# Last layer norm of a decoder layer: variance of four blocks computed on GpSimd over three slots, and a dequantisation factor in one operation

## Chip, cores and metric

One core of a Trainium2 chip runs the whole kernel in one launch. The metric is the device time of one execution in microseconds (us). Engines are named as in the profile: PE is TensorE (PEld its weight loads), DVE is VectorE, ACT is ScalarE, POOL is GpSimd, SP is SyncE, which here issues the DMAs.

## The reference, cut to what matters

The input is x (64, 64, 256) float32, so 4096 tokens of 256 values. Three parts follow each other, each with a residual and a layer norm. The change lies in the third:

```python
def _quant_weight(w):
    scale = jnp.mean(jnp.abs(w)) + EPS
    return jnp.clip(jnp.round(w / scale), -1.0, 1.0) * scale

def _quant_act(x):
    scale = jnp.maximum(jnp.max(jnp.abs(x), axis=-1, keepdims=True), EPS) / 127.0
    return jnp.clip(jnp.round(x / scale), -128.0, 127.0) * scale

def bitlinear(x, w):
    return jnp.einsum('bsi,oi->bso', _quant_act(x), _quant_weight(w))

x = _layernorm(x + self_attention(x))
x = _layernorm(x + cross_attention(x, ctx))
gate = sigmoid(bitlinear(x, w_gate))          # 256 -> 1024
h = gate * bitlinear(x, w_up)                 # 256 -> 1024
x = _layernorm(x + bitlinear(h, w_down))      # 1024 -> 256
# _layernorm(x) = (x - mean) / sqrt(var + 1e-5), over the 256 values of a token
```

## The kernel before

The tokens lie in SBUF as X, 32 blocks of 128 tokens (a token per partition) by 256 values. Self-attention and cross-attention run first (functions self_attention and cross_attention, about 1366 us of the span). The feed-forward (function feed_forward, from L1431) is the rest, and the change touches it alone.

It is written as one program per engine. Each is a loop over 36 slots (blocks, L1470), and in slot n an engine does the pieces of several blocks: has(k) says that block n-k exists. All orders are written out by hand; every engine works its own list strictly in that order, and a wait on a semaphore stops all that is behind it on that engine.

For block n the pieces are: PE multiplies into gP and uP (L1487, slot n); ACT takes the sigmoid of gP (sig, L1529, slot n); DVE multiplies by uP (hs, L1630), takes the largest magnitude (hsc, L1633) and its reciprocal (hinv, L1635), all in slot n; POOL limits hinv (L1581), quantises to hm (L1584) and makes the dequantisation factor dsc in two steps (L1585, L1587), in slot n; PE transposes hm (L1506) and ACT copies it out as hqT (L1540) in slot n+2; PE multiplies with the down weights into xprojP (L1497, called dP in the code), ACT scales that by dsc (ds, L1535) and POOL adds it to X (L1578) in slot n+3; DVE takes the norm's statistics (L1665, a count, a mean and a sum of squares for the even and the odd values) and aggregates them to mean and variance (ln_moments, L1667) in slot n+4. The last three blocks are scaled and added by DVE (L1661).

The normalisation works on groups of four blocks. POOL's roots (L1564 to L1571) makes 1/sqrt(var + eps) and minus mean times that, for the four blocks at once, in the slot in which the fourth is aggregated: for blocks 4m to 4m+3 that is slot 4m+7. ACT normalises block e in slot e+10 (L1554), as its last piece in that slot, after hqT of block n-2 and ahead of the next slot's sig. The first block of a group, 4m, is therefore normalised in slot 4m+10:

```python
NORMED = [[e for e in range(MAIN) if min(e + 10, NB + 3) == n] for n in range(NB + 4)]
for e in NORMED[n]:
    wait(act, s_shift, e // GROUP + 1)
```

MAIN is 28: blocks 28 to 31 form two groups of their own (28 to 30, and 31), normalised by DVE at the end (L1678). Blocks 28 to 31 also pass the norm of the cross-attention here, since their last projection ends as the feed-forward starts: DVE's L1638 to L1652, POOL's L1591 to L1603, and ACT's L1550, in slots 1 to 13. SP sends each finished group to the output (L1620).

DVE may write hs of block n once POOL's hm of block n-2 is done; PE may write uP of block n once hs of n-1 is done, and gP of n once sig of n-1 is done.

Of the kernel before, what the change touches and what calls it, by code (L numbers as in the profile page):

```python
# [5 lines left out]
F32 = mybir.dt.float32  # L6
# [1424 lines left out]
def feed_forward(nc, X, ffn, projP, out, sem, sb, part):  # L1431
# [11 lines left out]
    s_g, s_u, s_t, s_dn = (sem("f_" + n) for n in ("g", "u", "t", "dn"))  # L1443
    s_sig, s_h, s_max, s_sc, s_inv, s_dsc, s_hm, s_te, s_ds, s_y = (sem("f_" + n) for n in (
        "sig", "h", "max", "sc", "inv", "dsc", "hm", "te", "ds", "y"))
    s_stats, s_mom, s_rstd, s_normed, s_out = (sem("f_" + n) for n in ("stats", "mom", "rstd", "normed", "out"))
# [28 lines left out]
    with nc.Block() as block:  # L1475
# [46 lines left out]
        def _(act):  # L1522
            def slot(n, has):
# [35 lines left out]
        @block.gpsimd  # L1559
        def _(pool):  # L1560
            def roots(m):
                own = groups[m]
                wait(pool, s_mom, own.stop)
                nc.gpsimd.tensor_scalar(rstd[:, own], moments[:, own, 1], EPS, None, ALU.add).then_inc(s_small, 1)  # L1564
                wait(pool, s_small, 2 * m + 2 - max(0, m - MAIN // GROUP))
                nc.gpsimd.tensor_tensor(rstd[:, own], rstd[:, own], power[:, 0:own.stop - own.start], ALU.pow).then_inc(s_rstd, 1)
                if own.stop <= MAIN:
                    nc.gpsimd.tensor_scalar(shift[:, own], moments[:, own, 0], -1.0, None, ALU.mult).then_inc(s_small, 1)
                    wait(pool, s_small, 2 * m + 3)
                    wait(pool, s_rstd, m + 1)  # L1570
                    nc.gpsimd.tensor_tensor(shift[:, own], shift[:, own], rstd[:, own], ALU.mult).then_inc(s_shift, 1)  # L1571

            def slot(n, has):
# [5 lines left out]
                if has(0):  # L1579
                    wait(pool, s_inv, n + 1)  # L1580
                    nc.gpsimd.tensor_scalar(hinv[:, n:n + 1], hinv[:, n:n + 1], 1.0 / EPS, 127.0, ALU.min, ALU.mult).then_inc(s_sc, 1)  # L1581
                    wait(pool, s_sc, 2 * n + 1)
                    wait(pool, s_t, n - 1)
                    nc.gpsimd.tensor_scalar(hm[:, n % 2, :], hs[:, n % 2, :], hinv[:, n:n + 1], MAGIC16, ALU.mult, ALU.add).then_inc(s_hm, 1)  # L1584
                    nc.gpsimd.tensor_scalar(hsc[:, n:n + 1], hsc[:, n:n + 1], EPS, 1.0 / 127.0, ALU.max, ALU.mult).then_inc(s_sc, 1)  # L1585
                    wait(pool, s_sc, 2 * n + 2)
                    nc.gpsimd.tensor_tensor(dsc[:, n:n + 1], hsc[:, n:n + 1], wsc[:, 2:3], ALU.mult).then_inc(s_dsc, 1)  # L1587
                if n == 5:
# [35 lines left out]
        def _(dve):  # L1624
            def slot(n, has):
                if has(0):
                    wait(dve, s_sig, n + 1)
                    wait(dve, s_u, n + 1)
                    wait(dve, s_hm, n - 1)
                    nc.vector.scalar_tensor_tensor(hs[:, n % 2, :], uP[:, :], usc[:, n:n + 1], sig[:, n % 2, :],  # L1630
                                                   ALU.mult, ALU.mult).then_inc(s_h, 1)
                    wait(dve, s_h, n + 1)
                    nc.vector.tensor_reduce(hsc[:, n:n + 1], hs[:, n % 2, :], AX, ALU.max, apply_absolute_value=True).then_inc(s_max, 1)  # L1633
                    wait(dve, s_max, n + 1)
                    nc.vector.reciprocal(hinv[:, n:n + 1], hsc[:, n:n + 1]).then_inc(s_inv, 1)  # L1635
                if 1 <= n < 1 + PB:
# [94 lines left out]
```

## Time and profile before

| | us |
|---|---|
| median of 3 runs (lowest, highest) | 1492.27 (1491.41, 1496.97) |
| the profiled execution's own time | 1494.54 |
| its span | 1492.8 |
| mean granted clock of TensorE in it | 0.986 |
| busy over the span: PE, DVE, ACT, POOL | 1408.2, 1197.6, 1255.8, 1270.1 |
| of 1438 to 1452 us (14 us, in the feed-forward): PE, DVE, ACT, POOL | 14.00, 13.52, 12.87, 11.88 |

The profile is one execution, recorded per instruction; its times are counted from the start of the span. A timeline row gives the start, the duration, the engine, the line and what is written from what; a duration of an instruction in flight overlaps the next, so the cost of one on its engine is the distance from its start to the next one's start. "[1.96 <-ACT sig L1529]" behind a row means that its engine had stood idle for 1.96 us until that one finished.

### The profile page before, as it was taken

Reading aid. Unit: us, or ns where it says so; the run is one execution under the profiler, and the core shown is the slowest. Engines: PE = TensorE matmul, PEld = TensorE weight load, DVE = VectorE, ACT = ScalarE, POOL = GpSimd, SP = SyncE. Lnnn points to the kernel's source line nnn. Section 1 sums busy time; section 2 is a strip of 40 time slices with the busy share of each in tenths; the row PEclk is TensorE's granted clock in tenths of the full one; section 3 lists DMA queues with packets and bytes.
Section 4 is the critical chain, followed back from the end, with each engine's and each line's share of the span. In section 5 each row is a group of like instructions: output and inputs, shape, how many; then the busy total and the mean of one; then the engine's idle time right before and its main releaser. Section 6 shows DMA issues by size and latency. Waiting matters only on the chain. (4 is left out here: it accounts for less than half of the span.)

```text
span 1492.8 us, 54232 instructions
## 1 busy us (share of the span) xinstructions
PE 1408.2 (94%) x20034; PEld 1035.4 (69%) x20034; DVE 1197.6 (80%) x2796; ACT 1255.8 (84%) x4059; POOL 1270.1 (85%) x1307
## 2 busy tenths in 40 slices
PE   6999999999999999999999999778999999987897
PEld 4677777777777777777777777636777777765564
DVE  5887887887888878878877778777888888874997
ACT  6888888888888888888888887668999999995787
POOL 6989999999889889899898897657888899883887
PEclk9999999999999999999999999899999999998999
DMA  7700000000000000000000000022434433330012
GB/s 256 199 3 31 31 3 30 31 3 31 21 13 30 3 31 31 3 31 31 3 17 16 3 3 3 5 82 83 114 110 113 111 94 97 98 86 1 1 43 72
DMA packets 58133, 73.27 MB, mean 49 GB/s; under 512 B 14320, under 2 KB 41776, under 8 KB 57872
## 3 DMA queue, kind: packets, MB, share of 16 engines
q1 hardware_dynamic: 57872, 69.79, 15.6%
q8 instruction: 163, 2.67, 0.8%
q14 instruction: 98, 0.80, 0.2%
HBM read 32.54 MB, written 4.19 MB: 25 GB/s over the span
## 5 line engine op out<-in xcount | busy, mean ns | idle before, releaser
L652 DVE SCALAR_TENSOR_TENSOR X<-projP,r,X 128x256 f32<-128x256 f32 x512 | 211.2, 475 | 2.4 <-PE projP L333 2.3
L302 PEld LDWEIGHTS svP<-W,xT 128*128 128x128 bf16 x3072 | 182.2, 98 | 30.5 <-DVE scores L639 0.7
L256 PE MATMUL qkssP<-xT,W 128*128 128x512 bf16 x768 | 189.2, 383 | 9.2 <-POOL W L730 8.0
L725 POOL TENSOR_TENSOR y_sql<-y_sq 128x512 bf16<-128x512 f32 x128 | 133.5, 1043 | 71.5 <-ACT y_sq L457 71.2
L302 PE MATMUL svP<-W,xT 128*128 128x128 bf16 x3072 | 192.4, 219 | 0.0
L256 PE MATMUL kP<-xT,W 128*128 128x512 bf16 x768 | 186.9, 379 | 0.2 <-DVE kl L693 0.2
L333 PE MATMUL projP<-W,y 128*128 128x256 bf16 x1024 | 176.6, 275 | 2.1 <-POOL yl L725 2.1
L1216 ACT ACTIVATE x_probs<-xsP,x_ntop 128x64 f32<-128x64 f32 x512 | 152.2, 324 | 25.9 <-DVE x_ntop L1293 25.1
L472 ACT ACTIVATE probs<-scores,ntop 128x64 f32<-128x64 f32 x512 | 170.5, 339 | 3.7 <-DVE ntop L642 3.5
L725 POOL TENSOR_TENSOR k_sql<-moved_k 128x512 bf16<-128x512 f32 x128 | 135.8, 1061 | 19.2 <-ACT moved_k L483 18.1
L924 POOL TENSOR_TENSOR qhl<-qh 128x1024 bf16<-128x1024 f32 x64 | 121.2, 1893 | 33.3 <-issue 26.0
L765 POOL TENSOR_TENSOR KVl<-q 128x512 bf16<-128x512 f32 x128 | 145.6, 1137 | 0.0
L333 PE MATMUL projP<-W,yl 128*128 128x256 bf16 x512 | 140.5, 274 | 0.0
L256 PEld LDWEIGHTS kP<-xT,W 128*128 128x128 bf16 x768 | 75.2, 98 | 91.6 <-issue 0.8
L768 POOL TENSOR_TENSOR vl<-v 128x512 bf16<-128x512 f32 x128 | 135.6, 1059 | 0.7 <-DVE v L669 0.7
L725 POOL TENSOR_TENSOR q_sql<-turned_k 128x512 bf16<-128x512 f32 x128 | 133.1, 1040 | 2.9 <-ACT turned_k L464 2.9
L725 POOL TENSOR_TENSOR yl<-y 128x512 bf16<-128x512 f32 x128 | 133.1, 1040 | 0.0
L256 PEld LDWEIGHTS qkssP<-xT,W 128*128 128x128 bf16 x768 | 64.9, 98 | 77.1 <-issue 10.4
L669 DVE COPY v<-svP 128x512 f32<-128x512 f32 x128 | 88.3, 690 | 31.7 <-PE svP L302 31.2
L639 DVE SCALAR_TENSOR_TENSOR scores<-svP,r,bias 128x64 f32<-128x64 f32 x512 | 110.0, 277 | 4.5
L688 DVE TENSOR_TENSOR ptl<-pyP,pth 128x256 bf16<-128x256 f32 x128 | 54.3, 424 | 73.7 <-ACT pth L497 71.4
L1216 ACT ACTIVATION_READ_ACCUMULATOR x_probs<-xsP,x_ntop 128x1 f32 x512 | 111.4, 218 | 0.0
(277 smaller groups left out, 4934.6 us busy)
## 6 DMA issues: line engine op xcount, KB each, us to landing
x_turned<-x_turn SPq DMA_DIRECT2D x128, 128.0 KB, 2.1
oB<-oA SPq DMA_DIRECT2D x232, 64.0 KB, 2.0
w_stage<-in_wqkvp SPq DMA_DIRECT2D x16, 512.0 KB, 3.5
x_stage<-in_xT SPq DMA_DIRECT2D x8, 512.0 KB, 4.1
X<-in_x SPq DMA_DIRECT2D x1, 4096.0 KB, 16.9
x_stage<-in_ctxT SPq DMA_DIRECT2D x8, 512.0 KB, 4.4
out<-X SPq DMA_DIRECT2D x7, 512.0 KB, 2.9
okv<-in_L_xattn_W_o SPq DMA_DIRECT2D x1, 2048.0 KB, 11.5
```

The lines of the kernel that those rows point to most:

```text
L256: last = nc.tensor.matmul(dst[:, :], weight(parity, u, i, c), xT[:, z, c, tok], start=(c == 0 and k == 0), stop=(c == CC - 1 and k == 2))
L302: last = nc.tensor.matmul(svP[:, b * D:(b + 1) * D], xT[:, u, c, t * TILE + b * P:t * TILE + (b + 1) * P], weight(parity, z, 2, c), start= ...
L333: last = nc.tensor.matmul(projP[:, b * C:(b + 1) * C], y_part, W[:, (j - 3) // NT % 2, z, 3 * CC * D:], start=(i == 0), stop=(i == 2))
L472: last = nc.scalar.activation(probs[:, b, :], scores[:, b, :], ACT.Exp, bias=ntop[:, b:b + 1], accum_out=total[:, b:b + 1])
L639: last = nc.vector.scalar_tensor_tensor(scores[:, b, :], svP[:, b * T:(b + 1) * T], r[:, b:b + 1], row, ALU.mult, ALU.add)
L652: last = nc.vector.scalar_tensor_tensor(acc, projP[:, b * C:(b + 1) * C], r[:, PB + b:PB + b + 1], acc, ALU.mult, ALU.add)
L669: nc.vector.tensor_copy(v[:, j % 4, :], svP[:, :]).then_inc(s_ve, 1)
L725: return nc.gpsimd.tensor_tensor(dst[:, :], src[:, :], high(src, slice(None), 0, TILE), ALU.subtract)
L765: nc.gpsimd.tensor_tensor(ql[:, j % 2, :], q[:, j % 2, :], high_of(q, j % 2), ALU.subtract).then_inc(s_ql, 1)
L768: nc.gpsimd.tensor_tensor(vl[:, j % 4, :], v[:, j % 4, :], high_of(v, j % 4), ALU.subtract).then_inc(s_vl, 1)
L924: return eng.tensor_tensor(dst, src, high_part(src), ALU.subtract)
L1216: last = nc.scalar.activation(probs[:, m % 3, b % PB, b // PB, :], sP[:, b * T:(b + 1) * T], ACT.Exp, bias=ntop[:, b:b + 1], accum_out=tot ...
```

## The change

DVE no longer aggregates blocks 0 to 27 (L1667 remains for 28 to 31). POOL makes their variance out of the two halves' means and sums of squares: with M the mean of the even values, N of the odd, and S and T their sums of squares, 4 (var + eps) = (S + T) 4/C + 4 eps + (M - N)^2. For a group of four blocks this takes ten operations of 128x4, in three pieces: sums (three) in slot 4m+7, variances (four) in slot 4m+8, and roots (three) in slot 4m+9, which ends with the doubling of rstd that ACT's normalisation now waits for. ACT's list is as it was; the semaphore count that it waits for is that of the last operation of roots. Besides, 1/127 is multiplied into the weight's scale once (wdc), so that dsc takes one operation with two steps instead of two operations, in every slot. DVE's two semaphores of max and reciprocal become one that counts both.

```diff
+    gap, wdc = sb("ln3_gap", [P, NB], F32), sb("wdc", [P, 1], F32)
...
                 for e in NORMED[n]:
                     x = X[:, e, :]
-                    wait(act, s_shift, e // GROUP + 1)
+                    wait(act, s_shift, 2 * (e // GROUP + 1))
                     nc.scalar.activation(x, x, ACT.Identity, bias=shift[:, e:e + 1], scale=rstd[:, e:e + 1]).then_inc(s_by_act, 1)
...
+            def sums(m):
+                own = groups[m]
+                st = stats[:, own, :]
+                wait(pool, s_stats, own.stop)
+                nc.gpsimd.tensor_tensor(gap[:, own], st[:, :, 1], st[:, :, 4], ALU.subtract).then_inc(s_small, 1)
+                nc.gpsimd.tensor_tensor(shift[:, own], st[:, :, 1], st[:, :, 4], ALU.add).then_inc(s_small, 1)
+                nc.gpsimd.tensor_tensor(rstd[:, own], st[:, :, 2], st[:, :, 5], ALU.add).then_inc(s_small, 1)
+
+            def variances(m):
+                own = groups[m]
+                wait(pool, s_small, 7 * m + 5)
+                nc.gpsimd.tensor_scalar(rstd[:, own], rstd[:, own], 4.0 / C, 4.0 * EPS, ALU.mult, ALU.add).then_inc(s_small, 1)
+                nc.gpsimd.tensor_tensor(gap[:, own], gap[:, own], gap[:, own], ALU.mult).then_inc(s_small, 1)
+                nc.gpsimd.tensor_scalar(shift[:, own], shift[:, own], -1.0, None, ALU.mult).then_inc(s_small, 1)
+                wait(pool, s_small, 7 * m + 8)
+                nc.gpsimd.tensor_tensor(rstd[:, own], rstd[:, own], gap[:, own], ALU.add).then_inc(s_small, 1)
+
             def roots(m):
                 own = groups[m]
-                wait(pool, s_mom, own.stop)
-                nc.gpsimd.tensor_scalar(rstd[:, own], moments[:, own, 1], EPS, None, ALU.add).then_inc(s_small, 1)
...
+                wait(pool, s_small, 7 * m + 9)
+                nc.gpsimd.tensor_tensor(rstd[:, own], rstd[:, own], power[:, :], ALU.pow).then_inc(s_rstd, 1)
+                wait(pool, s_rstd, m + 1)
+                nc.gpsimd.tensor_tensor(shift[:, own], shift[:, own], rstd[:, own], ALU.mult).then_inc(s_shift, 1)
+                wait(pool, s_shift, 2 * m + 1)
+                nc.gpsimd.tensor_scalar(rstd[:, own], rstd[:, own], 2.0, None, ALU.mult).then_inc(s_shift, 1)
...
                 if has(0):
-                    wait(pool, s_inv, n + 1)
+                    wait(pool, s_top, 2 * n + 2)
...
-                    nc.gpsimd.tensor_scalar(hsc[:, n:n + 1], hsc[:, n:n + 1], EPS, 1.0 / 127.0, ALU.max, ALU.mult).then_inc(s_sc, 1)
-                    wait(pool, s_sc, 2 * n + 2)
-                    nc.gpsimd.tensor_tensor(dsc[:, n:n + 1], hsc[:, n:n + 1], wsc[:, 2:3], ALU.mult).then_inc(s_dsc, 1)
+                    nc.gpsimd.tensor_scalar(dsc[:, n:n + 1], hsc[:, n:n + 1], EPS, wdc[:, 0:1], ALU.max, ALU.mult).then_inc(s_dsc, 1)
...
                 for m in range(NG):
-                    if n - 4 == groups[m].stop - 1:
-                        roots(m)
+                    end = groups[m].stop - 1
+                    if end < MAIN:
+                        for lag, part_ in enumerate((sums, variances, roots)):
+                            if n - 4 - lag == end:
+                                part_(m)
+                    elif n - 4 == end:
+                        last_roots(m)
...
+            nc.gpsimd.tensor_scalar(wdc[:, :], wsc[:, 2:3], 1.0 / 127.0, None, ALU.mult).then_inc(s_small, 1)
...
                     nc.vector.bn_stats(stats[:, e, :], X[:, e, :]).then_inc(s_stats, 1)
-                    wait(dve, s_stats, e + 1)
-                    nc.vector.bn_aggr(moments[:, e, :], stats[:, e, :]).then_inc(s_mom, 1)
+                    if e >= MAIN:
+                        wait(dve, s_stats, e + 1)
+                        nc.vector.bn_aggr(moments[:, e, :], stats[:, e, :]).then_inc(s_mom, 1)
```

POOL's list before, from its last operation of slot 7 to the end of slot 8, with the first group's roots between (X<-ds,X opens a slot; dsc closes its part for the block):

```order
L1587 TENSOR_TENSOR dsc<-hsc,wsc 128x1 [waits f_sc]
L1564 TENSOR_SCALAR ln_rstd<-ln_moments 128x4 [waits f_mom]
L1566 TENSOR_TENSOR ln_rstd<-ln_rstd,ln_power 128x4 [waits f_small]
L1568 TENSOR_SCALAR ln_shift<-ln_moments 128x4
L1571 TENSOR_TENSOR ln_shift<-ln_shift,ln_rstd 128x4 [waits f_rstd,f_small]
L1578 TENSOR_TENSOR X<-ds,X 128x256 [waits f_ds]
L1581 TENSOR_SCALAR hinv<-hinv 128x1 [waits f_inv]
L1584 TENSOR_SCALAR hm<-hs,hinv 128x1024 [waits f_t,f_sc]
L1585 TENSOR_SCALAR hsc<-hsc 128x1
L1587 TENSOR_TENSOR dsc<-hsc,wsc 128x1 [waits f_sc]
```

POOL's list of the change over the end of slot 8 and slot 9, where the same group's second and third pieces stand (its sums stand at the end of slot 7):

```order
L1611 TENSOR_SCALAR hm<-hs,hinv 128x1024 [waits f_t,f_sc]
L1612 TENSOR_SCALAR dsc<-hsc,wdc 128x1
L1576 TENSOR_SCALAR ln_rstd<-ln_rstd 128x4 [waits f_small]
L1577 TENSOR_TENSOR ln_gap<-ln_gap 128x4
L1578 TENSOR_SCALAR ln_shift<-ln_shift 128x4
L1580 TENSOR_TENSOR ln_rstd<-ln_rstd,ln_gap 128x4 [waits f_small]
L1605 TENSOR_TENSOR X<-ds,X 128x256 [waits f_ds]
L1608 TENSOR_SCALAR hinv<-hinv 128x1 [waits f_top]
L1611 TENSOR_SCALAR hm<-hs,hinv 128x1024 [waits f_t,f_sc]
L1612 TENSOR_SCALAR dsc<-hsc,wdc 128x1
L1586 TENSOR_TENSOR ln_rstd<-ln_rstd,ln_power 128x4 [waits f_small]
L1588 TENSOR_TENSOR ln_shift<-ln_shift,ln_rstd 128x4 [waits f_rstd]
```

The last operation that ACT needs of the group (L1590, behind the row shown last) now stands behind the hm of two more slots than L1571 did.

ACT's list before, which the change leaves in this order, around the end of slot 9 and slot 10 (the row of L1554 is the first block of the first group):

```order
L1550 ACTIVATE X<-X,ln_shift,ln_rstd 128x256 [waits f_lastp]
L1529 ACTIVATE sig<-gP,gsc 128x1024 [waits f_h,f_g]
L1535 ACTIVATE ds<-xprojP,dsc 128x256 [waits f_y,f_dsc,f_dn]
L1540 ACTIVATE hqT<-hmP 128x1024 [waits f_dn,f_t]
L1554 ACTIVATE X<-X,ln_shift,ln_rstd 128x256 [waits f_shift]
```

Nothing moved there; the next row on ACT is the sig of slot 11.

## Rows read from the trace of the kernel before

**Rows 1.** Chain that ended last, a slot of the feed-forward: start, us, engine, what, line

```profile
1439.19 1.29 DVE hs L1630
...
1441.76 0.16 DVE hinv L1635
...
1442.39 1.30 DVE hs L1630
```

**Rows 2.** Timeline of DVE, the slot before: start us, us, engine, line, op, out<-in

```profile
1438.64 0.41 DVE L1665 BATCH_NORM_STATS2 ln_stats<-X 128x6 f32<-128x256 f32 x1
1439.08 0.18 DVE L1667 BATCH_NORM_AGGREGATE ln_moments<-ln_stats 128x2 f32<-128x6 f32 x1
```

**Rows 3.** Timeline of PE, first and fifth of the groups of one slot

```profile
1422.87 1.03 PE L1487 MATMUL gP<-wg,xqT 128*128 128x512 bf16 x4
...
1425.92 0.61 PE L1516 MATMUL hmP<-identh,f_xs 128*128 128x128 f16 x8
```

**Rows 4.** Timeline of POOL, slot 9 (an ordinary slot)

```profile
1406.14 0.72 POOL L1578 TENSOR_TENSOR X<-ds,X 128x256 f32<-128x256 f32 x1
1406.94 0.22 POOL L1581 TENSOR_SCALAR hinv<-hinv 128x1 f32<-128x1 f32 x1
1407.26 1.12 POOL L1584 TENSOR_SCALAR hm<-hs,hinv 128x1024 f16<-128x1024 f32 x1
1408.46 0.22 POOL L1585 TENSOR_SCALAR hsc<-hsc 128x1 f32<-128x1 f32 x1
1408.77 0.19 POOL L1587 TENSOR_TENSOR dsc<-hsc,wsc 128x1 f32<-128x1 f32 x1
1408.91 0.72 POOL L1578 TENSOR_TENSOR X<-ds,X 128x256 f32<-128x256 f32 x1
```

**Rows 5.** Timeline of POOL, roots of the first group, end of slot 7

```profile
1401.37 0.25 POOL L1564 TENSOR_SCALAR ln_rstd<-ln_moments 128x4 f32<-128x4 f32 x1
1401.70 1.04 POOL L1566 TENSOR_TENSOR ln_rstd<-ln_rstd,ln_power 128x4 f32<-128x4 f32 x1
1402.83 0.26 POOL L1568 TENSOR_SCALAR ln_shift<-ln_moments 128x4 f32<-128x4 f32 x1
1403.17 0.20 POOL L1571 TENSOR_TENSOR ln_shift<-ln_shift,ln_rstd 128x4 f32<-128x4 f32 x1
```

**Rows 6.** Timeline of ACT and DVE: block 0's normalisation in slot 10, then slot 11

```profile
1407.63 0.59 ACT L1554 ACTIVATE X<-X,ln_shift,ln_rstd 128x256 f32<-128x256 f32 x1
1408.12 1.10 ACT L1529 ACTIVATE sig<-gP,gsc 128x1024 f32<-128x1024 f32 x1
...
1409.38 1.28 DVE L1630 SCALAR_TENSOR_TENSOR hs<-uP,usc,sig 128x1024 f32<-128x1024 f32 x1
```

**Rows 7.** Timeline of ACT, DVE, POOL: the last tile's norm, slots 6 and 7

```profile
1394.93 0.60 ACT L1550 ACTIVATE X<-X,ln_shift,ln_rstd 128x256 f32<-128x256 f32 x1 [2.05 <-POOL ln_shift L1596]
...
1396.57 1.28 DVE L1630 SCALAR_TENSOR_TENSOR hs<-uP,usc,sig 128x1024 f32<-128x1024 f32 x1 [1.96 <-ACT sig L1529]
...
1399.39 0.23 POOL L1581 TENSOR_SCALAR hinv<-hinv 128x1 f32<-128x1 f32 x1 [0.99 <-DVE hinv L1635]
```

**Rows 8.** Timeline of DVE and POOL: hs of slots 12 and 15, f_xs in slot 12

```profile
1414.62 1.28 DVE L1630 SCALAR_TENSOR_TENSOR hs<-uP,usc,sig 128x1024 f32<-128x1024 f32 x1
...
1419.67 1.05 POOL L1603 TENSOR_SCALAR f_xs<-X,xinv 128x256 f16<-128x256 f32 x2
...
1425.62 1.28 DVE L1630 SCALAR_TENSOR_TENSOR hs<-uP,usc,sig 128x1024 f32<-128x1024 f32 x1 [0.32 <-ACT sig L1529]
```

**Rows 9.** Busy time by stretch (us, PE, PEld, DVE, ACT, POOL, then PE's granted clock, DMA)

```profile
1413.90:1415.97 2.07, 0.05 (x2) 0.01 (x1) 1.97 (x6) 1.73 (x3) 1.55 (x5) 1.00 0.00 0
...
1418.20:1419.20 1.00, 1.00 (x10) 0.88 (x9) 1.00 (x1) 0.50 (x2) 0.92 (x2) 0.50 0.00 0
...
1396.60:1398.00 1.40, 1.12 (x5) 0.39 (x6) 1.36 (x2) 1.40 (x3) 1.24 (x4) 1.00 0.00 0
```

**Rows 10.** Timeline of DVE: the last hs, slot 31

```profile
1478.05 1.28 DVE L1630 SCALAR_TENSOR_TENSOR hs<-uP,usc,sig 128x1024 f32<-128x1024 f32 x1
```

More of the change, by code:

```diff
@@ L1443, in feed_forward @@
     s_g, s_u, s_t, s_dn = (sem("f_" + n) for n in ("g", "u", "t", "dn"))
-    s_sig, s_h, s_max, s_sc, s_inv, s_dsc, s_hm, s_te, s_ds, s_y = (sem("f_" + n) for n in (
-        "sig", "h", "max", "sc", "inv", "dsc", "hm", "te", "ds", "y"))
+    s_sig, s_h, s_top, s_sc, s_dsc, s_hm, s_te, s_ds, s_y = (sem("f_" + n) for n in (
+        "sig", "h", "top", "sc", "dsc", "hm", "te", "ds", "y"))
     s_stats, s_mom, s_rstd, s_normed, s_out = (sem("f_" + n) for n in ("stats", "mom", "rstd", "normed", "out"))
@@ L1564, in roots, with last_roots @@
+            def last_roots(m):
+                own = groups[m]
+                wait(pool, s_mom, own.stop - MAIN)
                 nc.gpsimd.tensor_scalar(rstd[:, own], moments[:, own, 1], EPS, None, ALU.add).then_inc(s_small, 1)
-                wait(pool, s_small, 2 * m + 2 - max(0, m - MAIN // GROUP))
+                wait(pool, s_small, 7 * (MAIN // GROUP) + 3 + m - MAIN // GROUP)
                 nc.gpsimd.tensor_tensor(rstd[:, own], rstd[:, own], power[:, 0:own.stop - own.start], ALU.pow).then_inc(s_rstd, 1)
[L1567 to L1571, printed above, removed]
@@ L1579, in slot @@
                 if has(0):
-                    wait(pool, s_inv, n + 1)
+                    wait(pool, s_top, 2 * n + 2)
                     nc.gpsimd.tensor_scalar(hinv[:, n:n + 1], hinv[:, n:n + 1], 1.0 / EPS, 127.0, ALU.min, ALU.mult).then_inc(s_sc, 1)
-                    wait(pool, s_sc, 2 * n + 1)
+                    wait(pool, s_sc, n + 1)
                     wait(pool, s_t, n - 1)
                     nc.gpsimd.tensor_scalar(hm[:, n % 2, :], hs[:, n % 2, :], hinv[:, n:n + 1], MAGIC16, ALU.mult, ALU.add).then_inc(s_hm, 1)
-                    nc.gpsimd.tensor_scalar(hsc[:, n:n + 1], hsc[:, n:n + 1], EPS, 1.0 / 127.0, ALU.max, ALU.mult).then_inc(s_sc, 1)
-                    wait(pool, s_sc, 2 * n + 2)
-                    nc.gpsimd.tensor_tensor(dsc[:, n:n + 1], hsc[:, n:n + 1], wsc[:, 2:3], ALU.mult).then_inc(s_dsc, 1)
+                    nc.gpsimd.tensor_scalar(dsc[:, n:n + 1], hsc[:, n:n + 1], EPS, wdc[:, 0:1], ALU.max, ALU.mult).then_inc(s_dsc, 1)
                 if n == 5:
@@ L1604, in slot @@
                 for m in range(NG):
-                    if n - 4 == groups[m].stop - 1:
-                        roots(m)
+                    end = groups[m].stop - 1
[5 more added lines that the diff above has]
+                        last_roots(m)
             nc.gpsimd.memset(power[:, :], -0.5).then_inc(s_small, 1)
-            pool.wait_ge(s_small, 1)
+            nc.gpsimd.tensor_scalar(wdc[:, :], wsc[:, 2:3], 1.0 / 127.0, None, ALU.mult).then_inc(s_small, 1)
+            pool.wait_ge(s_small, 2)
             blocks(slot, 4)
@@ L1632, in slot @@
                     wait(dve, s_h, n + 1)
-                    nc.vector.tensor_reduce(hsc[:, n:n + 1], hs[:, n % 2, :], AX, ALU.max, apply_absolute_value=True).then_inc(s_max, 1)
-                    wait(dve, s_max, n + 1)
-                    nc.vector.reciprocal(hinv[:, n:n + 1], hsc[:, n:n + 1]).then_inc(s_inv, 1)
+                    nc.vector.tensor_reduce(hsc[:, n:n + 1], hs[:, n % 2, :], AX, ALU.max, apply_absolute_value=True).then_inc(s_top, 1)
+                    wait(dve, s_top, 2 * n + 1)
+                    nc.vector.reciprocal(hinv[:, n:n + 1], hsc[:, n:n + 1]).then_inc(s_top, 1)
                 if 1 <= n < 1 + PB:
```

## The prediction, made before the changed kernel had run

> **What bounds it now.** I read the page first: over the whole span PE is busiest, but the change touches only the feed-forward, so I cut that stage out. The chain of waits runs there through DVE alone in nearly every slot: hs at 1439.19, the reciprocal at 1441.76, the next hs at 1442.39 [rows 1]. A slot is thus 3.20 us, and DVE sets it. The timelines of the engines say how near the others are. PE needs 3.05 us when it waits for nothing (first gP at 1422.87, the fifth group at 1425.92 [rows 3]). POOL needs 2.77 us for an ordinary slot (1406.14 to 1408.91 [rows 4]) and once in four slots the roots: 1401.37 to 1403.17, and about 0.15 for the last of them, 1.95 us [rows 5]. So four slots cost POOL 4 x 2.77 + 1.95 = 13.03 us, against DVE's 12.80. **POOL is already slightly over DVE**, and only the one block by which hm may lag hides it.
>
> The last view is the one that decides: ACT's list. Block 0 is normalised at 1407.63, then comes sig of slot 11 at 1408.12, and DVE's hs of slot 11 at 1409.38 [rows 6]. The shift that this needs was written at 1403.37 (1403.17 + 0.20 [rows 5]), 4.26 us earlier. The normalisation stands in front of a sig, and sig feeds DVE. What happens when it is late is to be seen once: in slot 6 it waited 2.05 us for POOL's shift, and DVE's hs stood idle 1.96 us for the sig behind it [rows 7].
>
> **Part 1: 28 aggregates leave DVE.** Statistics start at 1438.64, the aggregate at 1439.08 [rows 2], the next hs at 1439.19 [rows 1]. Without the aggregate, hs could start 0.33 after the statistics (0.41, less the 0.08 by which independent DVE instructions overlap: hs starts 0.11 after the start of an aggregate of 0.18). DVE gains 0.22 a slot and needs 2.98. PE's 3.05 then stops it, so at most 0.15 a slot is to be had.
>
> **Part 2: dsc in one operation.** hsc and dsc take 0.31 + 0.14 = 0.45 (1408.46, 1408.77, 1408.91 [rows 4]). One operation of hsc's kind takes 0.30; if its end overlapped the next as dsc's does, 0.17. I take 0.30, since the two-step operations in the rows (hinv, hm, hsc) all show their whole duration and 0.08 behind it. It saves 0.15 a slot on POOL, 0.28 at best. The new wdc at the start is one such operation, at a time when POOL has nothing to do; the new waits of the kernel's start cost nothing.
>
> **Part 3: ten operations for four on POOL.** The power costs 1.13 (1401.70 to 1402.83 [rows 5]). Three operations with constants cost 0.33 each, 0.99 (1401.37 to 1401.70). Of the six with two tensors five are followed by one that does not need their result: 0.15 each, as dsc [rows 4]; the sixth, the shift, is waited for: 0.28 (0.20 and 0.08). That is 1.13 + 0.99 + 0.75 + 0.28 = 3.15 us a group, against 1.95. They read strided statistics, which no row shows; the upper bound is 0.28 for all six, 3.80 us. POOL's four slots become 4 x 2.62 + 3.15 = 13.63 us: it saved 0.60 and got 1.20.
>
> The Trainium skill speaks against this on its own ground: GPSIMD Engine Reference, section 3 (Performance versus the Vector engine), says that elementwise work belongs on VectorE, because a GpSimd instruction passes two software dispatch hops. The rows give it right here in the balance: 4 x 0.22 = 0.88 us off DVE for 1.20 us onto POOL. The rule alone would move the kernel by POOL's rate only, which is the first rival below.
>
> **Part 4: where roots now ends.** Follow POOL from the hinv of slot 7, whose time DVE sets: 1399.39 [rows 7]. The slots before it lose 0.37 (one aggregate 0.22 and one dsc 0.15 on that way), so 1399.02. From there POOL does hinv, hm, dsc (0.32 + 1.20 + 0.30 = 1.82), sums (0.45), slot 8 (X 0.80 + 1.82 = 2.62), variances (0.33 + 0.15 + 0.33 + 0.15 = 0.96), slot 9 (2.62), and roots to the end of the doubling (1.13 + 0.28 + 0.25 = 1.66): 10.13 us, which ends at **1409.15**. ACT would reach block 0 at 1407.63 at the latest. So it waits some 1.5 us or more. Behind the wait stand sig of slot 11, then hs on DVE, then uP of slot 12 on PE, then hinv and hm on POOL. hs of slot 11 starts 0.03 + 0.49 (normalisation to sig [rows 6]) + 1.13 (sig to hs, 0.03 the handover: as rows 7, where the ACT starts 0.03 after POOL's end) later, at 1410.80 against 1409.38: **+1.42 us**.
>
> This closes a ring, and the ring is longer than the slots it replaces. From the end of one group's roots to the end of the next: 0.03 + 0.49 + 1.13, then hs to the end of the reciprocal and over to POOL 2.76 (1439.19 to 1441.76 + 0.16 [rows 1], + 0.03), then POOL's 10.13. Sum **14.54 us per four slots**, against 12.80. From hs of slot 11 to that of slot 31 there are five such rings.
>
> The trace has 68.67 us there (1409.38 to 1478.05 [rows 6, 10]). Now: 5 x 14.54 = 72.70. In the first of them the f_xs of slots 12 and 13 come on POOL's way, 2 x 1.14 (1.05 + 0.09) = 2.28 [rows 8]. DVE's extra work in slot 11 (hs to hs 5.24 instead of 3.20 [rows 6, 8]) makes hinv of slot 12 ready 2.98 + 2.04 + 2.76 = 7.78 after hs of slot 11, when POOL is there at 2.76 + 1.82 + 0.45 + 0.80 = 5.83: 1.95 more. In the second, ACT's copy of the last tile delays a sig; I take 0.7 of its 0.9. Sum 72.70 + 2.28 + 1.95 + 0.7 = 77.63: **+8.96 us**. The tail after the last hs hardly changes: I take -0.2. The last group's roots end about a microsecond later, and their output is sent before the last one, which hides it; uncovered it would cost that microsecond.
>
> **The clock** of PE is the open term. After an idle stretch of 2.07 us it fell from 2.4 to 1.2 GHz (granted clock 0.50), and it did not fall after the 1.56 us ahead of 1396.6 [rows 9]. The rings leave PE idle about 1.6 us each, and the first, with DVE's and POOL's extra work, more. While low, PE's groups took 1.65 us more (gP 1.71 from start to start against 0.87, and less for the two before it); part of it is hidden by the ring. I add **1.0 us** for one such fall.
>
> Sum: 1.42 + 8.96 - 0.2 + 1.0 = **+11.2 us**. Against the profiled execution's own 1494.5 us that is 1505.7. This execution lies 2.3 us over the median of 1492.3, so for the median I say 1503.5 us, and 1504 rounded up for the strided reads.
>
> **Rivals.** What a measurement of this kernel can tell from no change is about 0.5%, 7.5 us.
>
> *POOL's rate alone (chance 0.10).* If ACT's wait were met in time, POOL would set the pace with 13.63 us per four slots, 0.83 over DVE's 12.80: over five to six groups 4 to 5 us, less what hm's lag absorbs at the start, so +3 to +4, or 1496. Against it: to be in time roots would have to end 1.5 us earlier, and all durations on that way are measured ones. This also covers the case that small POOL operations overlap much more than in the rows.
>
> *The gain comes through (0.03).* If the ten operations ran closely packed in POOL's gaps, at 0.1 each beside the power, POOL would need 4 x 2.5 + 2.0 = 12.0, and roots would end before ACT asks. The pace would be PE's 3.05, 0.15 under now, over 24 slots: -3.6 us, and 1488.7. It decides from the point at which POOL's way of 10.13 us falls below 8.6. No small row is as short as 0.1.
>
> *The clock falls in every ring (0.22).* The stalls of 1.6 us lie just under the one of 2.07 after which it fell. At 1.65 us a fall, half to all of it in the way, five falls add 4 to 8 us, less the 1.0 taken: 1507 to 1511. The Trainium skill bears on this: TensorE: Matmul & The Clock Gate, section HAM oscillation, says that a wait which comes back in every step makes the array start cold in every step, so that the price is paid each time. By it this rival would be the forecast; the row without a fall after 1.56 us keeps it below.
>
> **Numbers.** The forecast's own chance is 0.65: its lower bound is dsc at 0.17 (three on the ring, six rings, -2.3 us) and no fall (-1.0), so +8 us, 1500; its upper one is 0.28 for five more operations (six rings x 0.65 = +3.9), 1508. I give 1497 to 1511, which takes in the clock's rival and the upper part of POOL's rate. Slower by over 0.5% begins at 1499.7: forecast and clock, less a little for the low edge and the scatter of 1491.4 to 1497.0 in the runs, 0.83. Within 0.5%: 0.15. Faster: 0.02.
>
> **What the profile will show.** Right: in slots 10, 14, 18, 22, 26 and 30 the ACT row X<-X,ln_shift,ln_rstd waits 1.5 to 2.5 us for POOL's ln_rstd, and the hs of the next slot waits for sig; hs to hs is near 3.0 in three slots and about 5.3 in the fourth; the chain passes through POOL's hm, DVE no longer fills it. dsc reads 0.30 from start to start, the ten operations about 3.15. Wrong: no idle time ahead of ACT's normalisation, or a four-slot period under 13.2 us. If the period is 14.5 and the total is off, the clock's row in each stall tells the rest.

## The result, and the profile after

| | before | with the change |
|---|---|---|
| median, us (runs) | 1492.65 (4) | 1511.43 (4) |
| lowest, highest | 1491.41, 1496.97 | 1510.78, 1512.68 |
| profiled execution: own time, span | 1494.54, 1492.8 | 1512.68, 1509.2 |
| the same pair once more, on another chip, medians | 1496.15 (11) | 1510.19 (5) |

The ratio is 1.0112 with a 95% interval of 1.0090 to 1.0134; on the second chip it is 1.0098 (1.0083 to 1.0114). The change made the kernel slower, by 18.8 us in the first pair and by 14.0 in the second. The four runs of each kernel in the first pair do not overlap (1497.0 is the highest before, 1510.8 the lowest after).

The chain that ended last, by engine and by line, from the page of each kernel. DVE led it before:

```profile
DVE 5%; PE 1%; POOL 1%; issue 1%; ACT 0%; DVEq 0%; ACTq 0%; POOLq 0%
```

POOL leads it now:

```profile
POOL 5%; issue 2%; DVE 1%; PE 1%; ACT 0%; DVEq 0%; POOLq 0%; ACTq 0%
POOL hm L1611 2%; POOL X L1605 1%; POOL dsc L1612 1%; POOL hinv L1608 0%; POOL ln_rstd L1586 0%; PE xprojP L1498 0%; DVE hs L1661 0%; POOL f_xs L1628 0%; DVE hsc L1664 0%; ACT hqT L1541 0%; PE hmP L1507 0%; PE uP L1488 0%; POOL ln_shift L1578 0%; POOL ln_rstd L1590 0%; PE gP L1488 0%
```

The waits of the changed kernel from 1403 to 1493 us (engine and line, for whom, us in total, times, longest). ACT's normalisation waited for nothing before; now it waits six times, and the six sigs behind it are what DVE and PE wait for:

```profile
DVE hs L1661 <- ACT sig L1530: 18.9, 12, 4.8
ACT X L1555 <- POOL ln_rstd L1590: 14.8, 6, 4.6
...
PE gP L1488 <- ACT sig L1530: 9.7, 5, 2.7
POOL hinv L1608 <- DVE hinv L1666: 7.9, 7, 1.5
```

The first of these waits, in POOL's, ACT's and DVE's timelines. It stands where [rows 6] showed none:

```profile
1410.38 1.04 POOL L1586 TENSOR_TENSOR ln_rstd<-ln_rstd,ln_power 128x4 f32<-128x4 f32 x1
1411.49 0.20 POOL L1588 TENSOR_TENSOR ln_shift<-ln_shift,ln_rstd 128x4 f32<-128x4 f32 x1
1411.79 0.25 POOL L1590 TENSOR_SCALAR ln_rstd<-ln_rstd 128x4 f32<-128x4 f32 x1
...
1412.07 0.60 ACT L1555 ACTIVATE X<-X,ln_shift,ln_rstd 128x256 f32<-128x256 f32 x1 [2.16 <-POOL ln_rstd L1590]
1412.58 1.09 ACT L1530 ACTIVATE sig<-gP,gsc 128x1024 f32<-128x1024 f32 x1
...
1413.70 1.29 DVE L1661 SCALAR_TENSOR_TENSOR hs<-uP,usc,sig 128x1024 f32<-128x1024 f32 x1 [2.45 <-ACT sig L1530]
```

Roots end at 1412.04; 0.03 later ACT starts, 0.51 after that sig, 1.12 later hs. This is the hand-over that the last tile had shown in [rows 7], now in slots 10, 14, 18, 22, 26 and 30. The second wait is the longest, 4.55 us: the f_xs of slots 12 and 13 and DVE's extra work of slot 11 lie on POOL's way to it. The other five are 1.57 to 2.19 us.

**Where the loss lies.** The medians differ by 18.8 us, the two profiled executions by 18.1. I cut these two at DVE's addition of the last projection (the first row of the feed-forward on DVE, 1368.94 before and 1371.16 after), at hs of slot 0, 7, 11 and 31, and at the end. Every number is a difference of two starts of rows:

| stretch, us | before | changed | difference |
|---|---|---|---|
| start to the addition (no instruction differs) | 1368.94 | 1371.16 | +2.22 |
| addition to hs of slot 0 | 3.18 | 3.64 | +0.46 |
| hs 0 to hs 7 | 24.45 | 24.07 | -0.38 |
| hs 7 to hs 11 | 12.81 | 14.83 | +2.02 |
| hs 11 to hs 31, by fours | 16.24, 13.57, 12.82, 12.81, 13.23 | 18.89, 15.48, 14.82, 14.87, 14.83 | +10.22 |
| hs 31 to the end of the span | 14.75 | 16.61 | +1.86 |
| own time beyond the span | 1.74 | 3.48 | +1.74 |

The feed-forward itself (all but the first and the last row) is +14.18 us. The other 4 us lie outside it: 2.2 ahead of it, where no instruction differs, and 1.7 between the span and the execution's own time.

### The profile page after: what moved, and what is told of

It reads as the page before. It is cut to its first block and busy times, and to the rows that moved or that the text cites. A ratio compares the mean times of both kernels' runs of the same rounds, so it can differ in the third digit from the quotient of the medians.

```text
span 1509.2 us, 54004 instructions
## 1 busy us (share of the span) xinstructions
PE 1385.1 (92%) x19830; PEld 1037.3 (69%) x20034; DVE 1192.6 (79%) x2768; ACT 1255.5 (83%) x4059; POOL 1274.3 (84%) x1318
## 5 line engine op out<-in xcount | busy, mean ns | idle before, releaser
L256 PE MATMUL qkssP<-xT,W 128*128 128x512 bf16 x641 | 161.5, 383 | 29.9 <-issue 20.5
## 6 DMA issues: line engine op xcount, KB each, us to landing
x_turned<-x_turn SPq DMA_DIRECT2D x128, 128.0 KB, 2.1
```

Of the source, the lines that this page charges most:

```text
L256: last = nc.tensor.matmul(dst[:, :], weight(parity, u, i, c), xT[:, z, c, tok], start=(c == 0 and k == 0), stop=(c == CC - 1 and k == 2))
```

## The experiments

They ran in three series, each on a chip of its own. The kernel before has medians of 1497.45, 1496.15 and 1496.82 us there, about 4 us over the first pair's, so each run is compared with the kernel before that ran with it. First series: ACT's normalisation in slots e+11 and e+9 and the two halves alone (21 runs of the kernel before). Second: the change again, the two closer placements, the aggregates kept (11 runs). Third: the late aggregates and the factor alone again (29 runs). "Period" is the distance between the hs of slots 19 and 23, in the trace of each.

| run | ratio to before (95%) | median less before's | period | idle before ACT's normalisation |
|---|---|---|---|---|
| the kernel before | | | 12.82 | 0 |
| the change again | 1.0098 (1.0083 to 1.0114) | +14.0 | 14.82 | 14.8 |
| normalise in slot e+11 | 1.0025 (1.0016 to 1.0033) | +3.0 | 13.77 | 1.3 |
| normalise in slot e+9 | 1.0271 (1.0255 to 1.0287) | +41.6 | 19.63 | 34.3 |
| pieces all in slot 4m+7 | 1.0030 (1.0018 to 1.0043) | +4.6 | 13.87 | 1.1 |
| pieces in slots 4m+7, 4m+8 | 1.0039 (1.0026 to 1.0051) | +5.8 | 13.86 | 4.0 |
| slot e+11, aggregates kept | 1.0033 (1.0021 to 1.0045) | +4.4 | 13.79 | 0.8 |
| the norm's half alone | 1.0101 (1.0086 to 1.0116) | +15.3 | 15.35 | 16.7 |
| the factor's half alone | 0.9981 (0.9972 to 0.9989) | -2.9 | 12.82 | 0 |
| the factor alone, again | 0.9986 (0.9976 to 0.9996) | -1.9 | 12.81 | 0 |
| factor, and a late aggregate | 0.9986 (0.9975 to 0.9997) | -3.0 | 12.57 | 0 |
| late aggregate, old factor | 1.0006 (0.9996 to 1.0016) | +0.7 | 12.57 | 0.3 |

**The change once more.**

> The change itself, again, beside the kernel before on the chip of this series. In its first trace the feed-forward, from the last projection's addition to the end, took 138.04 us against 123.86, +14.2; the rest of the +18.8 us lay ahead of it (+2.2, where no instruction differs) and around the span. If that rest is chance of the execution and the chip, the pair differs here by 13 to 16 us; if it belongs to the change, by 18 to 20 again.

It is +14.0 us, and in its trace the feed-forward takes 138.3 us against 138.0 in the first (14.84, 18.89, 15.60, 14.82, 14.87, 14.82 from hs 7 to hs 31). That is the lower of the two expectations: 14 us belong to the change. What lay outside the feed-forward in the first pair did not come back; the addition starts anywhere between 1368.9 and 1373.2 in the traces of this study, whatever the kernel.

**ACT normalises one slot later.**

```diff
-            NORMED = [[e for e in range(MAIN) if min(e + 10, NB + 3) == n] for n in range(NB + 4)]
+            NORMED = [[e for e in range(MAIN) if min(e + 11, NB + 3) == n] for n in range(NB + 4)]
```

> The change, with ACT normalising block e one slot later (slot e+11). The work of all engines is the same. Ring theory (ACT waits for roots ahead of a sig): the ring loses one POOL slot of 2.6 us and falls from 14.83 to about 12.2 us per four slots, so it no longer sets the pace; no idle time ahead of ACT's normalisation of blocks 4m. POOL's own work then sets it, by the rows after the change 4 x 2.62 + 0.47 + 1.17 + 1.63 = 13.75 us per four slots, so about 1497 us, 14 us under the change, still 4 over the kernel before. Rival, POOL's load or the clock carries the loss and the wait is only where it shows: the order on ACT is of no account, 1509 to 1512 us. Second rival, the gain comes through once the wait is gone: under 1491.

The order of 28 instructions on ACT alone takes 11 of the 14 us away: +3.0 (I had expected +4). Nothing in the lists of DVE or POOL is different, so POOL's load did not carry those 11 us; it carries at most the 3 that are left. And the period is the predicted one, 13.75 expected and 13.76 to 13.77 measured. POOL's timeline of this kernel shows why: from the X that opens the slot after one group's roots to the same of the next it never stands idle (the ordinary slots between are left out, each 2.62 us):

```profile
1455.84 0.73 POOL L1605 TENSOR_TENSOR X<-ds,X 128x256 f32<-128x256 f32 x1
...
1461.10 0.20 POOL L1567 TENSOR_TENSOR ln_gap<-ln_stats 128x4 f32<-128x4 f32 x1
...
1463.92 0.30 POOL L1612 TENSOR_SCALAR dsc<-hsc,wdc 128x1 f32<-128x1 f32 x1
1464.30 0.20 POOL L1576 TENSOR_SCALAR ln_rstd<-ln_rstd 128x4 f32<-128x4 f32 x1
1464.58 0.20 POOL L1577 TENSOR_TENSOR ln_gap<-ln_gap 128x4 f32<-128x4 f32 x1
1464.87 0.24 POOL L1578 TENSOR_SCALAR ln_shift<-ln_shift 128x4 f32<-128x4 f32 x1
1465.19 0.20 POOL L1580 TENSOR_TENSOR ln_rstd<-ln_rstd,ln_gap 128x4 f32<-128x4 f32 x1
...
1467.96 1.04 POOL L1586 TENSOR_TENSOR ln_rstd<-ln_rstd,ln_power 128x4 f32<-128x4 f32 x1
1469.08 0.20 POOL L1588 TENSOR_TENSOR ln_shift<-ln_shift,ln_rstd 128x4 f32<-128x4 f32 x1
1469.37 0.24 POOL L1590 TENSOR_SCALAR ln_rstd<-ln_rstd 128x4 f32<-128x4 f32 x1
1469.59 0.73 POOL L1605 TENSOR_TENSOR X<-ds,X 128x256 f32<-128x256 f32 x1
```

1455.84 to 1469.59 is 13.75 us. DVE and PE now wait for POOL's hm, which is the second wait that the change brings once the first is gone. The waits of the same kernel from 1440 to 1481 us:

```profile
PEld hmP L1507 <- POOL hm L1611: 4.0, 5, 1.2
DVE hs L1661 <- POOL hm L1611: 3.6, 3, 1.2
```

**ACT normalises one slot earlier**, with e + 9 in the same line.

> The change, with ACT normalising block e one slot earlier (slot e+9). Ring theory: the ring grows by one POOL slot of 2.62 us, from 14.83 to 17.45 us per four slots; five rings and the first wait give 6 x 2.6 = 15.7 us, so 1527 us. If TensorE's clock also falls in each wait (they become 4.5 us), up to 1.65 us a ring come on top: 1527 to 1535. Rival, POOL's load carries the loss: no more than 1513 us.

The direction and the growth are the ring's, and a loss of +41.6 us has no place in the rival. The expectation of 1527 to 1535 was built on the first pair's change. Over the kernel before it is +34 to +42, which 41.6 just meets, but over the change it is +16 to +24, and measured against the change (+14.0) it is +27.6. The step from the change's rings to these explains that: 3.35, 3.75, 5.15, 4.81, 5.17 and 5.44 us from hs 7 to hs 31, together 27.7, where 2.62 each was to come from POOL's slot. The last three rings are 19.63 to 20.27 us instead of 17.45. The rest is PE. It stood idle for about 5 us in each ring (7.70 in the second), its clock fell each time, and then the chain ran through it. The chain in one ring (start us, us, what), and the granted clock (last but two) of two stretches of it:

```profile
1457.19 1.03 PE gP L1488 x2
...
1458.44 0.63 PE gP L1488
1459.08 1.71 PE uP L1488 x4
1460.78 1.23 PE xprojP L1498 x8
```

```profile
1457.00:1458.00 1.00, 0.81 (x2) 0.28 (x3) 0.83 (x1) 1.00 (x3) 0.42 (x1) 0.50 0.00 0
...
1459.00:1460.00 1.00, 1.00 (x4) 0.33 (x3) 0.97 (x3) 0.88 (x1) 0.00 (x1) 0.50 0.00 0
```

gP, uP and xprojP take 1.89 + 1.70 + 1.26 = 4.85 us there from gP's start to ds on ACT, against 3 x 0.87 = 2.61 at full clock, 2.2 more. 17.45 + 2.2 = 19.7.

**The three pieces closer together**, first all in slot 4m+7, then in slots 4m+7 and 4m+8, with ACT as in the change:

```diff
-                            if n - 4 - lag == end:
+                            if n - 4 == end:
```

> The change with all three pieces (sums, variances, roots) in slot 4m+7, ACT's order untouched (block e in slot e+10). Ring theory: roots is ready 2 slots earlier, no wait ahead of ACT's normalisation; POOL's load of 13.7 us per four slots stays and sets the pace against DVE's 12.8 before, so 3 to 5 us over the kernel before. Rival, the ten operations themselves cost what was lost and their place is of no account: 13 to 19 us over.

```diff
-                        for lag, part_ in enumerate((sums, variances, roots)):
+                        for lag, part_ in ((0, sums), (1, variances), (1, roots)):
```

> The change with sums in slot 4m+7 and variances and roots together in slot 4m+8, ACT's order untouched. Ring theory: roots is ready one POOL slot (2.62 us) earlier, the ring is 12.2 us and below POOL's 13.7, so POOL sets the pace: 3 to 5 us over the kernel before, as with ACT's later normalisation. Rival as in the one-slot run: 13 us or more over.

Both took the ring away from POOL's side, as the first did from ACT's: +4.6 and +5.8 us, the second a little above the 3 to 5 that I gave (its ACT still waits 4.0 us in sum). Ten operations in a row cost 3.38 us in the one-slot kernel (1459.55 to 1462.93 in its trace, sums to the next X), and 4 x 2.62 + 3.38 = 13.86 is its period. So with ACT's list as it is, the spreading over three slots cost 8 to 9 of the 14 us, and it brought POOL 0.1 us a group. The 4.6 us that remain in the one-slot kernel and the 3.0 of the later normalisation cannot be told apart: the intervals overlap, and in the two traces the feed-forward takes 128.2 and 128.0 us.

**The aggregates kept as extra work on DVE**, with ACT in slot e+11 (nothing reads what 28 of them write; a semaphore count that follows from it is left out):

```diff
-                    if e >= MAIN:
-                        wait(dve, s_stats, e + 1)
-                        nc.vector.bn_aggr(moments[:, e, :], stats[:, e, :]).then_inc(s_mom, 1)
+                    wait(dve, s_stats, e + 1)
+                    nc.vector.bn_aggr(moments[:, e, :], stats[:, e, :]).then_inc(s_mom, 1)
```

> The change with ACT normalising in slot e+11, and DVE's 28 aggregates put back as extra work that nothing reads. If POOL sets the pace there (13.76 us per four slots) DVE's 0.22 us a block is worth nothing: the same time as without them, 3 us over the kernel before, and 13.76 again. If DVE's shorter slot was worth something, up to 24 x 0.22 = 5 us slower than that: 8 us over.

+4.4 us against +3.0 without them, in two series, with overlapping intervals (1.0021 to 1.0045 and 1.0016 to 1.0033). The periods are alike (13.79, 13.76 and 14.11 against 13.77, 13.76, 13.76). DVE's 0.22 us a block is worth nothing that the period shows where POOL paces; a difference of a microsecond is open (in its trace two down projections of the tail ran at the low clock, in that of the kernel without them one).

**Each half alone.** The norm without the new factor (of its edit, the lines of the factor), then the new factor on the kernel before, which is the factor's part of the change:

```diff
-                    nc.gpsimd.tensor_scalar(dsc[:, n:n + 1], hsc[:, n:n + 1], EPS, wdc[:, 0:1], ALU.max, ALU.mult).then_inc(s_dsc, 1)
+                    nc.gpsimd.tensor_scalar(hsc[:, n:n + 1], hsc[:, n:n + 1], EPS, 1.0 / 127.0, ALU.max, ALU.mult).then_inc(s_sc, 1)
+                    wait(pool, s_sc, 2 * n + 2)
+                    nc.gpsimd.tensor_tensor(dsc[:, n:n + 1], hsc[:, n:n + 1], wsc[:, 2:3], ALU.mult).then_inc(s_dsc, 1)
```

> The change without its second half: POOL computes the variance in three pieces, the dequantisation factor stays two operations. Ring theory: each ring contains three factors more at 0.16 us, 14.83 becomes 15.3 us, six rings give +2.9 us on the change: 1514 us. Rival, the factor's operation is what costs in the change: 1505 or less.

> The kernel before with the dequantisation factor in one operation and nothing else. Both theories: POOL saves 0.16 us a slot and needs 12.4 us per four slots against DVE's 12.8, so DVE goes on setting the pace; only the first slots and the one wait of hs at slot 30 gain, 0.3 to 1 us: 1491.5 to 1493 us. If the two-step operation with its scalar from memory were the slow part of the change it would be 1495 or more.

The norm alone has a period of 15.35 us, 0.53 over the change, where three factors of 0.16 give 0.48. Its time is +15.3, which is 1.3 over the change in the other series; I had given 2.9 over the first pair's, whose 18.8 held 4 us of chance.

The factor alone gave -2.9 us, more than the 0.3 to 1 that I had allowed. The period is DVE's unchanged 12.81 to 12.82, so it is not there. In its trace hs 11 to hs 15 takes 14.83 us in place of 16.24, 1.41 less. PE's wait of slot 12 and its clock, in this kernel:

```profile
1418.84 1.04 PE L1488 MATMUL uP<-wu,xqT 128*128 128x512 bf16 x4 [1.74 <-DVE hs L1630]
...
1420.00:1422.00 2.00, 2.00 (x19) 1.26 (x17) 1.93 (x7) 1.21 (x2) 1.71 (x4) 1.00 0.01 4
```

Before, that wait was 2.02 us and the clock fell behind it (0.50 in [rows 9]); here it is 1.74 and the clock stays. What shortened the wait is one small instruction of DVE. In the kernel before it takes 0.69 us, and it ends 0.03 us after a hm of POOL that was under way when it started (POOL's row, then DVE's):

```profile
1412.81 1.12 POOL L1584 TENSOR_SCALAR hm<-hs,hinv 128x1024 f16<-128x1024 f32 x1
...
1413.27 0.69 DVE L1646 TENSOR_SCALAR xsc<-xsc 128x4 f32<-128x4 f32 x1
```

With the factor in one operation POOL starts that hm earlier (3.15 us behind hs of slot 11 instead of 3.43), and the same instruction takes 0.41 us; again it ends 0.03 us after the hm:

```profile
1415.69 1.12 POOL L1585 TENSOR_SCALAR hm<-hs,hinv 128x1024 f16<-128x1024 f32 x1
...
1416.43 0.41 DVE L1646 TENSOR_SCALAR xsc<-xsc 128x4 f32<-128x4 f32 x1
```

The 0.28 us between them are those of the wait, and of hs 11 to hs 12 (4.96 instead of 5.24). The other 1.13 lie in hs 13 to hs 15 (3.94 and 3.59 before, 3.20 and 3.20 now), behind the place where the clock fell. That the clock cost them is likely and was not isolated; there is one trace of the kernel before. The second run of the factor alone has 1.74, no fall, 14.84 and -1.9 us. So about 1.4 us of the factor's gain comes from where two instructions meet in one slot, and not from the pace.

> The factor in one operation alone, again, on this chip beside the two others: 2 to 3 us under the kernel before, as in the first series (ratio 0.998). Its four-slot period there was DVE's unchanged 12.81 us; the gain came from the stretch of slots 11 to 15, where TensorE's wait was 1.74 us in place of 2.02 and its clock did not fall. 0 to 1 us if that was chance.

It is -1.9 us, at the lower edge of the 2 to 3 expected; the interval (0.9976 to 0.9996) excludes that there is no gain.

**A version that takes less from DVE without giving POOL more.** The aggregate waits for its own statistics. Put one slot later, ahead of the next block's, it need not wait (this edit stands on the kernel before; the factor's part is left out):

```diff
+                    if 1 <= e <= MAIN:
+                        wait(dve, s_stats, e)
+                        nc.vector.bn_aggr(moments[:, e - 1, :], stats[:, e - 1, :]).then_inc(s_mom, 1)
                     wait(dve, s_y, e + 1)
                     nc.vector.bn_stats(stats[:, e, :], X[:, e, :]).then_inc(s_stats, 1)
-                    wait(dve, s_stats, e + 1)
-                    nc.vector.bn_aggr(moments[:, e, :], stats[:, e, :]).then_inc(s_mom, 1)
+                    if e >= MAIN:
+                        wait(dve, s_stats, e + 1)
+                        nc.vector.bn_aggr(moments[:, e, :], stats[:, e, :]).then_inc(s_mom, 1)
...
-                    if n - 4 == groups[m].stop - 1:
+                    if n - 4 == groups[m].stop - 1 + (groups[m].stop <= MAIN):
```

> The kernel before with the dequantisation factor in one operation, and with DVE aggregating each of blocks 0 to 27 one slot later, just ahead of the next block's statistics (POOL's roots one slot later too, in slot 4m+8). DVE's aggregate then waits for nothing: it should cost 0.11 us in place of the 0.22 it costs behind its own statistics (0.33 without, 0.55 with). DVE's four slots fall from 12.81 to about 12.4 us, where POOL stands at 12.43 (4 x 2.62 + 1.95). Six to seven groups gain 0.4: 2.4 us under the version with the factor alone, 5 us under the kernel before. Rival, the roots one slot later makes ACT wait as in the change: the shift was ready 4.26 us before its use, one slot takes 2.6 of it, so no wait; if there is one, the period is longer than 12.8. Second rival, the aggregate costs DVE the same wherever it stands: no gain on the factor alone.

> The same late aggregate with the dequantisation factor still in two operations. DVE needs 12.4 us for four slots, but POOL needs 13.03, so POOL sets the pace: no faster than the kernel before (12.81, where hm's lag hid the difference for a while), 0 to 1.5 us slower. If DVE alone counted, 2 to 3 us faster.

DVE's timeline with the new factor, in one slot:

```profile
1441.86 0.16 DVE L1635 RECIPROCAL hinv<-hsc 128x1 f32<-128x1 f32 x1
1441.94 0.16 DVE L1666 BATCH_NORM_AGGREGATE ln_moments<-ln_stats 128x2 f32<-128x6 f32 x1
1442.02 0.39 DVE L1668 BATCH_NORM_STATS2 ln_stats<-X 128x6 f32<-128x256 f32 x1
1442.53 1.28 DVE L1630 SCALAR_TENSOR_TENSOR hs<-uP,usc,sig 128x1024 f32<-128x1024 f32 x1
```

The aggregate costs DVE 0.08 us there (1441.94 to 1442.02), not 0.22. But the statistics are followed by an idle stretch (0.51 to the next hs, where 0.33 would do), and the chain of that kernel runs through PE's matmuls. The period is 12.57 instead of the 12.4 that I gave, and the time -3.0 us, with a ratio that cannot be told from that of the factor alone in the same series (both 0.9986). With the old factor it is +0.7, as POOL's 13.03 us said: its periods grow from 12.57 over 12.71 to 13.09 as the lag of hm is used up. So the factor's half of the change is worth keeping; about 2 to 3 us are what it is worth on the whole, and whether the late aggregate adds a microsecond is not settled by 12 runs.

## Why the prediction was right in kind and short in size

**The sign, the mechanism and the places were right.** ACT waits in the six slots named, for the doubling of rstd; the sig behind it makes hs late; POOL leads the chain. The main forecast was a ring of 14.54 us; it is 14.84 (mean of the last three). One sign was off: I wrote waits of 1.5 to 2.5 us in all six slots, and the second is 4.55. The sum had the extra work that makes it long, the sign had not.

**The size.** 1504 was forecast for the median, with 1497 to 1511; 1511.4 came, 0.4 above the upper end. Measured as a difference on one chip, it is +14.0 us against my +11.2. By terms:

| term | forecast | trace |
|---|---|---|
| first wait, to hs 11, with the first slots | +1.42 | +1.64 (-0.38 and +2.02) |
| hs 11 to hs 31 | +8.96 | +10.22 |
| tail | -0.2 | +1.86 |
| clock | +1.0 | nothing to be seen in hs 11 to hs 31; contained in the tail |
| hs of slot 0 | 0 | +0.46 |

*Part 2* was right: the factor went from 0.45 to 0.26 start to start, with 0.03 more ahead of it: 0.16 saved, 0.15 said. *Part 3*: the sixth operation's waits were right, the strided reads cost nothing (0.20 each, 0.16 from start to start). Short was the seam between the pieces. The way that POOL goes for one ring, in the changed kernel's timeline:

```profile
1465.71 0.22 POOL L1608 TENSOR_SCALAR hinv<-hinv 128x1 f32<-128x1 f32 x1 [1.15 <-DVE hinv L1666]
1466.09 1.12 POOL L1611 TENSOR_SCALAR hm<-hs,hinv 128x1024 f16<-128x1024 f32 x1 [0.15 <-POOL hinv L1608]
1467.31 0.29 POOL L1612 TENSOR_SCALAR dsc<-hsc,wdc 128x1 f32<-128x1 f32 x1
...
1475.85 0.24 POOL L1590 TENSOR_SCALAR ln_rstd<-ln_rstd 128x4 f32<-128x4 f32 x1
```

It is 1465.71 to 1476.09, 10.38 us; I had 10.13. hm to dsc is 1.22 to 1.23 where I carried over the 1.20 of hm to hsc. Behind dsc a TENSOR_SCALAR starts after 0.39 (1470.38 to 1470.77), not after 0.30. The variances took 1.04 (1470.77 to 1471.81), not 0.96, and the first hm starts 0.38 behind hinv, not 0.32. Two dsc ahead of instructions with two tensors took 0.26 and won some of it back. That is the mis-sized term of the ring, 0.25 of its 0.30, and it comes back in five rings and the first wait.

*The tail* was the step that failed. I wrote that it hardly changes, -0.2 us, and it took 1.86 more. But the sixth ring ends in it: ACT waits in slot 30, and PE then stands idle for 3.09 us and falls to half its clock for two blocks' down projections, 1.66 and 1.89 us instead of 1.05:

```profile
1493.88 1.66 PE L1498 MATMUL xprojP<-wd,hqT 128*128 128x256 bf16 x8 [3.09 <-ACT hqT L1541]
...
1497.52 1.89 PE L1498 MATMUL xprojP<-wd,hqT 128*128 128x256 bf16 x8 [1.12 <-ACT hqT L1541]
...
1501.37 1.05 PE L1498 MATMUL xprojP<-wd,hqT 128*128 128x256 bf16 x8 [1.12 <-ACT hqT L1541]
```

The two cost 0.61 + 0.84 = 1.45 of the 1.86. There nothing hides them, since from slot 31 on every hqT waits for PE and PE for hqT. Other kernels with ACT's order untouched agree: the tail takes 15.37 and 15.87 us where no down projection of it runs slow (the two closer placements), 16.85 and 17.02 where two or three do (the norm's half alone, the change again).

*The clock* was taken for one fall and fell twice: after an idle stretch of 2.75 us at 1432.6 and after the one of 3.09. It did not fall after 1.83, 1.24, 1.90 and 1.95 in the other rings. The +1.0 stood for a fall in the first rings, and that one cost nothing that shows: its ring (hs 15 to hs 19) took 15.48 us, where the ring of 14.84 and the 0.7 for ACT's copy give 15.54. The price was paid in the tail, where I had put nothing. So the rival in which it falls in every ring did not come in the change; it came in the kernel that normalises in slot e+9, after stretches of 4.91 to 7.70 us; the ring looked at above paid 2.2 us for it.

I had written that by the Trainium skill (TensorE: Matmul & The Clock Gate, section HAM oscillation) this rival would be the forecast. That read the page too widely: it tells of a kernel whose waits are 3 to 5 us, and the prediction put the rings' at 1.6. The trace agrees with the page in the kernel of slot e+9; the change's rings lie outside its case.

*Rival "POOL's rate alone"* is what remains when the ring is taken away: 13.76 us a period and +3.0 us, as its text said (+3 to +4). That the total fits is in part luck. In the trace of that kernel hs 7 to hs 31 takes only 1.2 us more than before (82.66 against 81.48, since hs 11 to hs 15 takes 14.18 instead of 16.24), and the tail 3.0 more (17.71 against 14.75), where the rival had nothing. The rule of the Trainium skill that elementwise work belongs on VectorE (GPSIMD Engine Reference, section 3) is thus worth 3 to 5 us of the 14, net of what the factor gives back. The rest is the order. *Rival "the gain comes through"* is out: even with the ring gone the kernel is not faster, and DVE's saving can be put back for nothing that the period shows.

The whole-kernel number moved by 4 us more than the feed-forward in the first pair. That was no step of mine, and it did not come back in the second pair: the terms of the feed-forward alone would have ended near 1507, inside the range. The runs of the kernel before had spread from 1491 to 1497, and the range had no room for that on top of its terms.

## What to carry to other kernels

When work moves to a later slot on one engine, look in the lists of the other engines for the instruction that needs it, and for what is queued behind that instruction: here a normalisation that nobody hurries for stood ahead of a sigmoid that everyone waits for, and 11 of the 14 us hung on 4.3 us of slack that the old order had. Sum the way from the end of the moved work back to itself as a ring and compare it with the period; put the consumer later by as much as the ring is too long. Here the producer had moved two slots; one slot for the consumer was enough, since the slack covered the rest. And work taken from the engine that sets the pace is worth only what the next engine allows, which here was less than nothing, because the next engine got the work.

## What the runs showed of the hardware that I had not expected

- A small DVE instruction was held up by POOL. The TENSOR_SCALAR on xsc (128x4) takes 0.17 us in the three traces in which no POOL instruction was under way at its start. In the ten others it takes 0.37 to 0.72 us, and each time it ends 0.02 to 0.03 us after that POOL instruction (nine times hm, once X). The traces show the coincidence of the ends, not its reason.
- TensorE's clock went with small differences of its idle time: behind a stretch of 2.02 us in slot 12 it fell to 0.50 (one trace), behind 1.74 in the same place (the factor alone, both traces) it stayed. Single stretches of 1.24 to 1.95 left it up in the rings of the change, those of 2.75, 3.09 and 5.05 did not. It is not the length of one stretch alone that decides, though. In the kernel with the norm's half alone the clock stayed up behind 2.35 and 2.42 us (at 1411.72 and 1462.25) and fell behind 2.43 (0.55 in the stretch of 1478.5 to 1479.5). With the late aggregate and the old factor it fell at 1429.9 us behind two stretches of 0.79 and 1.11 us, close to each other.
- On POOL a TENSOR_SCALAR of 128x1 whose second scalar is read from memory takes 0.30 us, 0.08 more than with two constants (0.22). The next instruction with two tensors starts 0.04 before its end (1410.11 to 1410.38 in the change), while one with constants starts 0.09 behind it (1470.38 to 1470.77).
- DVE's aggregate costs 0.22 us directly behind its own statistics ([rows 2]: 0.55 from the statistics to hs, 0.33 without it) and 0.08 one slot later (1441.94 to 1442.02).
